# Resident embedding tables as float32 lookups in a DLRM tower: twelve tables, eight for all tiles, four behind the first, one looped body

## The chip, the core and the metric

The kernel runs on one core of a Trainium2 chip. The metric is the device time of one execution in microseconds. Three executions of the kernel before took 177.21, 178.31 and 182.38 us, with a median of 178.31 us. TensorE (PE) multiplies, VectorE (DVE) and ScalarE (ACT) work element by element and empty the PSUM banks, GpSimd (POOL) issues the indirect gathers, and SyncE (SP) issues the plain loads.

## The reference

For 512 samples, 26 ids pick one row of 128 float32 values each from 26 tables (eight tables of 1,000 rows, nine of 1,250, eight of 12,500, one of 125,000). With the dense row that makes 27 vectors a sample. All 351 pairwise products of them, and the dense features twice, go through a small network:

```
e = stack([tbl_0[ids[:, 0]], ..., tbl_25[ids[:, 25]]], axis=1)          # 512 x 26 x 128
combined = concatenate((dense[:, None, :], e), axis=1)                  # 512 x 27 x 128
inter = einsum('bfd,bgd->bfg', combined, combined)[:, iu, ju]           # 512 x 351, pairs f < g
h = concatenate([dense, inter, dense], axis=1)                          # 512 x 607
h = maximum(h @ W_top1 + b_top1, 0)      # 607 x 512
h = maximum(h @ W_top2 + b_top2, 0)      # 512 x 256
y = h @ W_top3                           # 256 x 1
```

## The kernel before

The batch is worked in four tiles of 128 samples. Each tile needs its 27 vectors with the features on the partitions (`xT`, two buffers). They come from two sources.

**Gathered tables.** For 19 tables, GpSimd issues one indirect load a table and tile (L260, 76 in all): 128 rows into `emb`. TensorE turns each by a transpose (L297), and DVE or ACT copies it into `xT` (L420 to L423, L501).

**Resident tables.** Seven small tables lie whole in SBUF (`table`, 125 partitions of 8 rows). A lookup is a product of table rows with a one-hot mask. SP loads each table's ids broadcast to 125 partitions (L232) and then the table itself (L233), in turn for the seven. ACT casts the ids (L537), DVE compares them with each partition's row number (L432, 8 masks a table), and DVE splits the table exactly into three bfloat16 parts (L449 `rest`, L454 `low`). TensorE adds three passes of 8 bfloat16 products (L284), and ACT keeps the result in `known` (L527). `LOOKUPS` gives the order: the seven tables for the first tiles before tile 0, and six shorter lookups for the remaining samples between the steps of tiles 0 to 2.

A tile then runs so: 128 small products of 32 x 32 (L342), interrupted by transposes of the next tile and by the dense part of layer 1 (L308); DVE transposes in blocks (L470), DVE and ACT pick the pairs (L477, L560), TensorE turns them three times (L361), and layer 1 (L308, 12 products), layer 2 (L385, 8) and the last layer (L393, 2) follow. `FILL` says between which of these steps the next tile's transposes stand. `keep_busy` (L316) multiplies the identity by itself to keep TensorE running. All code is unrolled; the order on each engine is the order in which it is written.

## Time and profile before

| | |
|---|---|
| time, median of three | 178.31 us |
| span of the profiled execution | 136.7 us |
| what lies around the span (median less span) | 41.6 us |
| first product of tile 0 | 64.67 us |
| first product of tile 1 | 85.26 us |
| first product of tile 3 | 121.42 us |
| last copy of the result | 134.83 us |
| TensorE busy | 104.4 us |
| GpSimd busy, with 76 gathers | 79.7 us |

The profile shows one execution from the first to the last instruction of the program. The profiled execution's own device time is not recorded, so the median of the three stands for it, and the 41.6 us around the span are a difference of two executions. A product of float32 operands stands in the trace as two instructions of TensorE, one of bfloat16 operands and a transpose as one. Products overlap in the array, so their pace is read from the distance of their starts, not from the duration of one.

### The profile page before, as it was taken

To read this page: it belongs to the slowest core of one execution; us is meant where nothing else is said; L and a number is where in the kernel's file an instruction comes from. 1 tells how busy PE (TensorE), PEld (TensorE's weight loads), DVE (VectorE), ACT (ScalarE), POOL (GpSimd) and SP (SyncE) were. 2 spreads that over 40 slices of the span, in tenths; PEclk is the share of its full clock that TensorE was granted. 3 is DMA by queue.
4 is the path that set the end of the run, shared out by engine and by line. 5 is a ranking of instruction groups with operands and counts; after the bars stand their busy time and mean duration, and the time that the engine had idled before them with its cause. 6 is when DMAs were issued, how large, how long until landed. Compare 5 with 4: busy or idle time off the path is not lost.

```text
span 136.7 us, 3746 instructions
## 1 busy us (share of the span) xinstructions
PE 104.4 (76%) x1660; PEld 79.8 (58%) x1660; DVE 54.4 (40%) x134; ACT 31.9 (23%) x71; POOL 79.7 (58%) x84
## 2 busy tenths in 40 slices
PE   5606999694739849079749999969999399986594
PEld 5502344242315626057639998858987399766592
DVE  0076758584855346179322032240411314113211
ACT  4010103030302005551000383004730023530211
POOL 6777887878778787778777777777772000000000
PEclk9985699999986986856985699999999869999999
DMA  2544444444448787744212212222221000000000
GB/s 43 103 167 145 164 148 152 158 151 164 150 163 252 192 218 196 174 136 142 79 46 62 58 48 53 62 58 50 50 64 44 0 5 0 0 5 5 5 0 1
DMA packets 5866, 12.68 MB, mean 93 GB/s; under 512 B 1636, under 2 KB 2148, under 8 KB 5850
## 3 DMA queue, kind: packets, MB, share of 16 engines
q1 hardware_dynamic: 3274, 7.45, 17.0%
q0 software_dynamic: 2432, 4.99, 14.6%
q8 instruction: 13, 0.21, 0.6%
q10 hardware_dynamic: 144, 0.01, 0.1%
q14 instruction: 3, 0.02, 0.1%
HBM read 12.43 MB, written 0.00 MB: 91 GB/s over the span
## 4 chain that ended last, share of the span: by engine, by line
PE 45%; SPq 21%; DMA 17%; issue 10%; ACT 5%; DVE 1%; ACTq 0%
DMA ids_i<-in_resident_ids 17%; SPq L233 12%; PE bank L308 12%; SPq L232 9%; PE prod L342 9%; PE prod L284 6%; PE prod L385 5%; PE bank L284 5%; PE bank L297 5%; ACT xT L544 1%; PE bank L393 1%; ACT xT L513 1%; PE prod L361 1%; PE bank L316 1%; PE bank L361 1%
## 5 line engine op out<-in xcount | busy, mean ns | idle before, releaser
L260 POOL DMA_INDIRECT emb<-in_tbl,ids_sb x76 | 77.7, 1022 | 23.1 <-issue 22.5
L284 PE MATMUL prod<-mask,table 125*128 125x512 bf16 (+3 forms) x80 | 15.9, 352 | 18.3 <-issue 12.7
L432 DVE TENSOR_SCALAR mask<-ids_h,col_sb 125x512 bf16<-125x512 f16 (+1 forms) x72 | 19.1, 344 | 11.5 <-ACT ids_h L537 11.5
L284 PEld LDWEIGHTS prod<-mask,table 125*128 125x128 bf16 x80 | 7.4, 109 | 25.6 <-issue 17.0
L284 PE MATMUL prod<-mask,rest 125*128 125x512 bf16 (+3 forms) x80 | 15.9, 354 | 0.2 <-DVE rest L449 0.2
L449 DVE TENSOR_TENSOR rest<-table 125x1024 f32<-125x1024 f32 (+1 forms) x8 | 8.6, 1091 | 15.4 <-DMA table<-in_tbl 15.4
L537 ACT CAST ids_h<-ids_i 125x512 f16<-125x512 int32 x7 | 4.3, 618 | 44.6 <-DMA ids_i<-in_resident_ids 44.6
L342 PE MATMUL prod<-xT 128*32 128x32 f32 x1024 | 12.4, 199 | 2.9 <-issue 2.4
L284 PE MATMUL prod<-mask,low 125*128 125x512 bf16 (+3 forms) x80 | 14.0, 326 | 0.0
L342 PEld LDWEIGHTS prod<-xT 128*32 128x32 f32 x1024 | 10.6, 109 | 4.7 <-issue 3.3
L284 PEld LDWEIGHTS prod<-mask,rest 125*128 125x128 bf16 x80 | 8.2, 116 | 7.0 <-issue 2.8
L308 PE MATMUL bank<-pairs,w1p_sb 117*128 117x128 f32 x96 | 12.1, 286 | 0.0
L297 PE MATMUL bank<-ident,emb 128*128 128x128 f32 x76 | 12.1, 297 | 0.0
L308 PEld LDWEIGHTS bank<-pairs,w1p_sb 117*128 117x128 f32 x96 | 11.9, 204 | 0.0
L284 PEld LDWEIGHTS prod<-mask,low 125*128 125x128 bf16 x80 | 7.7, 108 | 5.0 <-DVE low L454 0.2
L470 DVE STREAM_TRANSPOSE inter_s<-prod 128x288 f32<-128x288 f32 (+1 forms) x8 | 4.6, 612 | 14.4 <-PE prod L342 14.4
L297 PEld LDWEIGHTS bank<-ident,emb 128*128 128x128 f32 x76 | 10.0, 158 | 0.4 <-issue 0.2
L454 DVE TENSOR_TENSOR low<-rest 125x1024 bf16<-125x1024 f32 (+1 forms) x8 | 8.6, 1090 | 0.6
L513 ACT COPY xT<-known 128x896 f32<-128x896 f32 (+1 forms) x4 | 7.5, 1872 | 3.3 <-DMA known<-in_dense_t 3.3
L316 PE MATMUL bank<-ident 128*128 128x128 f32 x28 | 5.8, 374 | 3.1 <-issue 1.6
L385 PE MATMUL prod<-h,w_sb 128*128 128x128 f32 x64 | 7.9, 276 | 0.0
L385 PEld LDWEIGHTS prod<-h,w_sb 128*128 128x128 f32 x64 | 7.5, 192 | 0.1
(46 smaller groups left out, 77.9 us busy)
## 6 DMA issues: line engine op xcount, KB each, us to landing
table<-in_tbl SPq DMA_DIRECT2D x7, 500.0 KB
ids_i<-in_resident_ids SPq DMA_DIRECT2D x7, 250.0 KB
emb<-in_tbl,ids_sb POOLq DMA_INDIRECT x76, 3.6
w1p_sb<-in_w_pairs SPq DMA_DIRECT2D x1, 702.0 KB
w1d_sb<-in_w_dense SPq DMA_DIRECT2D x1, 512.0 KB, 20.8
w_sb<-in_w SPq DMA_DIRECT2D x1, 512.0 KB
known<-in_dense_t SPq DMA_DIRECT2D x1, 256.0 KB, 22.2
ids_sb<-in_ids SPq DMA_DIRECT2D x1, 38.0 KB, 2.1
```

What stands on the lines that cost most here:

```text
L232: sp.dma_start(ids_i[:, r, :], resident_ids[r].partition_broadcast(part_rows)).then_inc(s_idb[r], 16)
L233: sp.dma_start(table[:, r, :], resident[r].rearrange("(p k) d -> p (k d)", k=ROWS_PER_PART)).then_inc(s_table[r], 16)
L260: nc.gpsimd.indirect_dma_start(out=emb[:, t % 2, f, :], out_offset=None, in_=gathered[f], in_offset=bass.IndirectOffsetOnAxis(ap=ids_sb[:, ...
L284: mm = nc.tensor.matmul(look_dst(n), src[:, k, :], mask[:, r % KEPT, k, samples], start=(part == 0 and k == 0), stop=(part == 2 and k == R ...
L297: mm = nc.tensor.transpose(t_bank[g][:, i * P:(i + 1) * P], emb[:, t % 2, f, :], ident[:])
L308: return nc.tensor.matmul(l1_bank[n // 2][:, (n % 2) * P:(n % 2 + 1) * P], weights[:, n * P:(n + 1) * P], x, start=(weights is w1_sum and ...
L342: mm = nc.tensor.matmul(prod[SLOT_PITCH * q:SLOT_PITCH * (q + 1), i, :], x, x, start=True, stop=True)
L385: mm = nc.tensor.matmul(l2_bank[m][:, 0:P], w2_sb[:, c, m * P:(m + 1) * P], h1[:, c, :], start=(c == 0), stop=(c == HID1 // P - 1))
L432: nc.vector.tensor_scalar(mask[:, r % KEPT, k, samples], ids_h[:, r % 2, samples], col_sb[0:part_rows, ROW_ID + k:ROW_ID + k + 1], None, A ...
L449: nc.vector.tensor_tensor(by_row(rest[:, r % KEPT, :])[:, ks], by_row(table[:, r, :])[:, ks], upper_halves(table[:, r, :])[:, ks], ALU.sub ...
L454: nc.vector.tensor_tensor(low[:, r % KEPT, ks], by_row(rest[:, r % KEPT, :])[:, ks], upper_halves(rest[:, r % KEPT, :])[:, ks], ALU.subtra ...
L513: nc.scalar.copy(slots(t, 0, n), known[:, 0:n, t * P:(t + 1) * P].rearrange("d f (q j) -> d q j f", q=QUADS)).then_inc(s_pack_known, 1)
```

## The change

Twelve small tables are resident instead of seven: the eight of 1,000 rows (`EARLY`) and four of 1,250 rows (`LATE`), padded to whole rows of 128 partitions. The early eight are looked up for all 512 samples before tile 0. The late four are gathered by GpSimd for tile 0 and looked up for the other 384 samples at the end of tile 0. Fourteen tables stay gathered, so there are 18 gathers for tile 0 and 14 for each other tile, 60 in all.

A lookup multiplies the float32 table rows by a float32 mask: 8 products a table (10 for a late one), with no split of the table. After the first two tables, tables go in pairs, and one mask instruction of DVE serves both. The ids of the first six tables are loaded as six rows, and six products with a broadcast identity spread them over the partitions; ACT copies the result out of PSUM to int16. The ids of the other six come by a broadcast load.

TensorE's work of a tile is a loop body that is run four times, with branches for what differs between tiles. `xT` has one buffer instead of two, products are 27 x 27, all of a tile's products stand in one run, and the weights come in one load.

```diff
-RESIDENT = 7
...
+EARLY, LATE = 8, 4
+RESIDENT = EARLY + LATE
...
+COLUMNS = LATE + GATHERED
+FIRST_SLOT = 1 + EARLY
+
+FIRST_GROUPS = [(0, 4), (4, 4), (8, 4), (12, 4), (16, 2)]
+LATER_GROUPS = [(4, 4), (8, 4), (12, 3), (15, 2), (17, 1)]
+NG = 5
...
+
+PAIRS = [(r, r + 1) for r in range(0, RESIDENT, 2)]
+EARLY_PAIRS = EARLY // 2
+MASKS = 6
 
...
-WARM_UP = 9
-BUSY_BEFORE_PAIRS, BUSY_AMONG_PAIRS = 2, 3
+EARLY_GROUPS = [[0], [1], [2, 3], []]
...
+SPREAD = 6
...
+WARM_UP, WARM_KEEP = 2, 4
...
-            for r in range(RESIDENT):
-                sp.dma_start(ids_i[:, r, :], resident_ids[r].partition_broadcast(part_rows)).then_inc(s_idb[r], 16)
-                sp.dma_start(table[:, r, :], resident[r].rearrange("(p k) d -> p (k d)", k=ROWS_PER_PART)
-                             ).then_inc(s_table[r], 16)
-            sp.dma_start(known[:, 0, :], dense_t).then_inc(s_dense, 16)
-            sp.dma_start(w1d_sb[:], w1_dense.rearrange("(c p) n -> p c n", p=P)).then_inc(s_w1d, 16)
-            sp.dma_start(w1p_sb[0:K_PAIRS], w1_pairs.rearrange("(k p) n -> p k n", p=K_PAIRS)).then_inc(s_w1p, 16)
-            sp.dma_start(w2_sb[:], w2.rearrange("(c p) n -> p c n", p=P)).then_inc(s_w2, 16)
-            sp.wait_ge(s_y, TILES)
+            n = single * D
+            for r in range(2):
+                sp.dma_start(resident(r), early[0][:, r * n:(r + 1) * n]).then_inc(s_table[r], 16)
+            for b in range(1, EARLY_PAIRS):
+                if 2 * b == SPREAD:
+                    sp.dma_start(ids_h[:, SPREAD:, :], other_ids.partition_broadcast(P)).then_inc(s_other_ids, 16)
+                    sp.dma_start(known[:, 0, :], dense_t).then_inc(s_dense, 16)
+                sp.dma_start(table[:, b, 0:2 * n_rows[2 * b] * D], early[b]).then_inc(s_table[1 + b], 16)
+            sp.dma_start(w_sb[:], weights).then_inc(s_w, 16)
+            for r in range(EARLY, RESIDENT):
+                sp.dma_start(resident(r), late[r - EARLY].rearrange("(p k) d -> p (k d)", p=P)
...
+                        pool.wait_ge(s_tr, NG * (t - 2) + turned[-1] + 1)
+                    for c in range(first, first + n):
                         nc.gpsimd.indirect_dma_start(
-                            out=emb[:, t % 2, f, :], out_offset=None, in_=gathered[f],
-                            in_offset=bass.IndirectOffsetOnAxis(ap=ids_sb[:, t, f:f + 1], axis=0),
-                        ).then_inc(s_gather[t % 2][g], 16)
+                            out=rows(t, c), out_offset=None, in_=gathered[c],
+                            in_offset=bass.IndirectOffsetOnAxis(ap=ids_sb[:, column + c:column + c + 1], axis=0),
+                        ).then_inc(s_gather[t % 2][g] if t else s_gather_first[g], 16)
...
-            def look_up(n):
...
-                pe.wait_ge(s_table[r], 16)
-                for part in range(3):
-                    src = [upper_halves(table[:, r, :]), upper_halves(rest[:, r % KEPT, :]), low[:, r % KEPT]][part]
-                    for k in range(ROWS_PER_PART):
...
-                        mm = nc.tensor.matmul(look_dst(n), src[:, k, :], mask[:, r % KEPT, k, samples],
-                                              start=(part == 0 and k == 0),
-                                              stop=(part == 2 and k == ROWS_PER_PART - 1))
-                mm.then_inc(s_look, 1)
+            def look_up_first():
+
+                for r in range(2):
+                    pe.wait_ge(s_table[r], 16)
+                    for k in range(single):
+                        pe.wait_ge(s_mask, r * single + k + 1)
+                        nc.tensor.matmul(looked(r), resident(r)[:, k * D:(k + 1) * D], made_single(r, k),
+                                         start=(k == 0), stop=(k == single - 1)).then_inc(s_used, 1)
+
+            def look_up(b):
+
+                n = n_rows[2 * b]
+                pe.wait_ge(s_table[1 + b], 16 if b < EARLY_PAIRS else 32)
+                for k in range(n):
+                    step = first_step[b] + k
+                    pe.wait_ge(s_mask, masks_to(step + 1))
+                    for r in PAIRS[b]:
+                        mm = nc.tensor.matmul(looked(r), resident(r)[:, k * D:(k + 1) * D],
+                                              made(step, b)[:, r % 2, :], start=(k == 0), stop=(k == n - 1))
+                    mm.then_inc(s_used, 1)
...
+                with nc.tensor.If(p == 2):
+                    for g in some:
+                        bank_free(g)
+                        pe.wait_ge(s_gather[0][g], 16 * LATER_GROUPS[g][1])
+                        turn(2, g)
+                with nc.tensor.Else():
+                    with nc.tensor.If(p < TILES):
+                        for g in some:
+                            bank_free(g)
+
+                            pe.wait_ge(s_gather[1][g], (p + 1) * (8 * LATER_GROUPS[g][1]))
+                            turn(1, g)
...
+            pe.wait_ge(s_ident, 1)
+            keep_busy(WARM_UP)
+
+            pe.wait_ge(s_row_of, 1)
+            pe.wait_ge(s_id_exact, 1)
+            for r in range(SPREAD):
+                nc.tensor.matmul(id_bank[r][:], row_of[:, r, :], id_exact[:], start=True, stop=True
+                                 ).then_inc(s_spread, 1)
+            keep_busy(WARM_KEEP)
+            look_up_first()
...
+            for b in range(EARLY_PAIRS):
+                if b >= 2:
+
+                    pe.wait_ge(s_known, 2 * b - 2)
+                if b >= 1:
+                    look_up(b)
+                for g in EARLY_GROUPS[b]:
+                    turn_first(g)
+
+            pe.wait_ge(s_known, 6)
+            pe.wait_ge(s_w1sum, 1)
+            dense_part(slice(0, P))
+            turn_first(NG - 1)
+
+            with nc.tensor.Fori(1, TILES + 1) as p:
+
+
+                pe.wait_ge(s_ready_act, p)
+                pe.wait_ge(s_ready_dve, p)
...
                     for q in range(QUADS):
-                        x = xT[:, t % 2, i, q, :]
-                        mm = nc.tensor.matmul(prod[SLOT_PITCH * q:SLOT_PITCH * (q + 1), i, :], x, x,
+                        x = xT[:, i, q, 0:SLOTS]
+                        mm = nc.tensor.matmul(prod[SLOT_PITCH * q:SLOT_PITCH * q + SLOTS, i, 0:SLOTS], x, x,
                                               start=True, stop=True)
                 mm.then_inc(s_prod, 1)
...
+                turn_next(p, (0, 1))
...
+                turn_next(p, (2, 3))
...
+                with nc.tensor.If(p < TILES):
+                    dense_part(bass.ds((p % TILES) * P, P))
+                turn_next(p, (4,))
+                with nc.tensor.If(p == 1):
+
+                    pe.wait_ge(s_pack[2], 2)
+                    pe.wait_ge(s_pack[3], 2)
+                    pe.wait_ge(s_h2_act, 1)
+                    pe.wait_ge(s_h2_dve, 1)
+                    for b in range(EARLY_PAIRS, len(PAIRS)):
+                        look_up(b)
+
+                    pe.wait_ge(s_known, 8)
...
+                nc.vector.tensor_scalar(made_single(r, k), ids_h[:, r, :], col_sb[:, row:row + 1], None,
+                                        ALU.is_equal).then_inc(s_mask, 1)
+
+            def make_mask(b, k):
+                step = first_step[b] + k
+                if step >= MASKS:
+                    dve.wait_ge(s_used, masks_to(step - MASKS + 1))
+                row = row_id[n_rows[2 * b]] + k
+                nc.vector.tensor_scalar(made(step, b), ids_h[:, 2 * b:2 * b + 2, samples(b)],
+                                        col_sb[:, row:row + 1], None, ALU.is_equal).then_inc(s_mask, 1)
...
-                for ks in parts:
-                    nc.vector.tensor_tensor(by_row(rest[:, r % KEPT, :])[:, ks], by_row(table[:, r, :])[:, ks],
-                                            upper_halves(table[:, r, :])[:, ks], ALU.subtract
-                                            ).then_inc(s_rest, 2 // len(parts))
-                for ks in parts:
-                    dve.wait_ge(s_rest, 2 * r + (1 if ks.stop < ROWS_PER_PART else 2))
-                    nc.vector.tensor_tensor(low[:, r % KEPT, ks], by_row(rest[:, r % KEPT, :])[:, ks],
-                                            upper_halves(rest[:, r % KEPT, :])[:, ks], ALU.subtract
-                                            ).then_inc(s_low, 2 // len(parts))
...
+                    dve.wait_ge(s_other_ids, 16)
+                    dve.wait_ge(s_w, 16)
+                    nc.vector.tensor_tensor(w1_sum[:], w_sb[:, W1D:W1D + HID1], w_sb[:, W1D + HID1:W1D + 2 * HID1],
+                                            ALU.add).then_inc(s_w1sum, 1)
```

TensorE's program ahead of tile 0, before (`prod` and `bank` are PSUM, `mask` the one-hot operand, `table`, `rest` and `low` the three parts of the resident rows):

```order
L316 MATMUL bank<-ident 128x128 x9
L284 MATMUL prod<-mask,table 128x512 x8
L284 MATMUL prod<-mask,rest 128x512 x8
L284 MATMUL prod<-mask,low 128x512 x8
...
L284 MATMUL prod<-mask,table 128x384 x8
...
L297 MATMUL bank<-ident,emb 128x128 x16
...
L284 MATMUL prod<-mask,table 128x256 x8
```

and now, up to the loop (`id_exact` and `row_of` are the ids and the broadcast identity):

```order
L341 MATMUL prod<-ident 128x128 x2
L349 MATMUL bank<-id_exact,row_of 128x512 x6
L341 MATMUL prod<-ident 128x128 x4
L281 MATMUL bank<-mask,table 128x512 x16
L299 MATMUL bank<-ident,emb 128x128 x4
L292 MATMUL prod<-mask,table 128x512 x16
...
L299 MATMUL bank<-ident,emb 128x128 x8
L292 MATMUL prod<-mask,table 128x512 x16
L330 MATMUL bank<-known,w_sum 128x128 x4
L299 MATMUL bank<-ident,emb 128x128 x2
```

Where 24 bfloat16 products made a lookup there are 8 float32 ones, all of 512 columns, 64 in this stretch. On TensorE, from tile 0's products on, before (tile 1's round):

```order
L342 MATMUL prod<-xT 32x32 x64
L284 MATMUL bank<-mask,table 128x128 x8
L284 MATMUL bank<-mask,rest 128x128 x8
L284 MATMUL bank<-mask,low 128x128 x8
L361 MATMUL bank<-ident,pairs_s 117x128
...
L385 MATMUL prod<-h,w_sb 128x128 x8
L297 MATMUL bank<-ident,emb 128x128 x7
L393 MATMUL bank<-h,col_sb 1x128 x2
```

and now the end of the loop body (the first branch leads past what stands under it unless the pass is that of tile 0):

```order
L412 COMPARE_AND_BRANCH
L292 MATMUL bank<-mask,table 128x384 x20
L292 MATMUL prod<-mask,table 128x384 x20
L412 UNCONDITIONAL_BRANCH
L424 MATMUL bank<-h,col_sb 1x128 x2
L369 REGISTER_ALU
L369 COMPARE_AND_BRANCH
```

The lookups that lay in short pieces between the steps of tiles 0 to 2 are now one block of 40 products behind tile 0's layer 2. SP's queue, before (from its second load) and now:

```order
L232 DMA ids_i<-in_resident_ids 125x512
L233 DMA table<-in_tbl 125x1024
...
L235 DMA known<-in_dense_t 128x512
L236 DMA w1d_sb<-in_w_dense 128x2x512
L237 DMA w1p_sb<-in_w_pairs 117x3x512
L238 DMA w_sb<-in_w 128x4x256
```

```order
L239 DMA table<-in_early 128x1024 x2
L244 DMA table<-in_early 128x2048 x2
L242 DMA ids_h<-in_other_ids 128x3072
L243 DMA known<-in_dense_t 128x512
L244 DMA table<-in_early 128x2048
L245 DMA w_sb<-in_weights 128x3584
L247 DMA table<-in_late 128x1280 x4
```

The loads that went to 125 partitions go to 128, and the broadcast of the ids shrinks from seven loads to one.

## Rows read from the trace of the kernel before

**Rows 1.** The page: span, and busy time of each engine.
```profile
span 136.7 us, 3746 instructions
PE 104.4 (76%) x1660; PEld 79.8 (58%) x1660; DVE 54.4 (40%) x134; ACT 31.9 (23%) x71; POOL 79.7 (58%) x84
```
**Rows 2.** Chain that ended last, in order of time: start us, length us, what.
```profile
30.08 22.72 DMA ids_i<-in_resident_ids
...
64.67 0.69 PE prod L342 x46
...
121.42 1.34 PE prod L342 x87
...
134.83 0.25 ACT y_row L578
```
**Rows 3.** Windows: stretch, length, engines busy, PEclk, DMA share, GB/s.
```profile
6.00:36.00 30.00, 21.58 (x92) 9.33 (x93) 20.00 (x43) 4.31 (x8) 23.60 (x22) 0.89 0.46 157
42.00:45.00 3.00, 3.00 (x15) 1.60 (x14) 1.57 (x7) 1.00 (x2) 2.25 (x3) 0.72 0.92 268
```
**Rows 4.** Timeline: the start of TensorE's work (start us, us, engine, line).
```profile
1.52 4.21 PE L316 MATMUL bank<-ident 128*128 128x128 f32 x18 [1.52 <-POOL ident L248]
...
11.31 3.17 PE L284 MATMUL prod<-mask,table 125*128 125x512 bf16 x7 [5.58 <-DMA table<-in_tbl]
```
**Rows 5.** Timeline, TensorE: bfloat16 lookups of 512 and of 384 columns.
```profile
18.98 1.89 PE L284 MATMUL prod<-mask,table 125*128 125x512 bf16 x8
20.70 1.89 PE L284 MATMUL prod<-mask,rest 125*128 125x512 bf16 x8
...
34.06 1.46 PE L284 MATMUL prod<-mask,rest 125*128 125x384 bf16 x8
35.38 1.48 PE L284 MATMUL prod<-mask,low 125*128 125x384 bf16 x8
```
**Rows 6.** Timeline: 128 columns in bfloat16, float32, one-column weights (last: its group).
```profile
100.28 0.61 PE L284 MATMUL prod<-mask,rest 125*128 125x128 bf16 x8
100.73 0.61 PE L284 MATMUL prod<-mask,low 125*128 125x128 bf16 x8
...
129.19 2.84 PE L308 MATMUL bank<-pairs,w1p_sb 117*128 117x128 f32 x24
...
133.98 0.38 PE L393 MATMUL bank<-h,col_sb 128*1 128x128 f32 x2
...
L393 PE MATMUL bank<-h,col_sb 128*1 128x128 f32 x16 | 2.7, 271 | 0.1
```
**Rows 7.** The gathers: their group on the page, the first and the last one.
```profile
L260 POOL DMA_INDIRECT emb<-in_tbl,ids_sb x76 | 77.7, 1022 | 23.1 <-issue 22.5
...
3.10 1.10 POOL L260 DMA_INDIRECT emb<-in_tbl,ids_sb  x1 [0.28 <-DMA ids_sb<-in_ids]
...
102.70 0.94 POOL L260 DMA_INDIRECT emb<-in_tbl,ids_sb  x1 [0.30 <-issue]
```
**Rows 8.** TensorE's instruction loads, and stretches of the chain with nothing waited for.
```profile
q8 instruction: 13, 0.21, 0.6%
...
105.75 2.35 issue
...
122.77 1.26 issue
...
126.24 1.63 issue
```
**Rows 9.** DVE and ACT by line and form: busy us, mean ns.
```profile
L432 DVE TENSOR_SCALAR mask<-ids_h,col_sb 125x512 bf16<-125x512 f16 x40 | 12.4, 380 | 8.7 <-ACT ids_h L537 8.7
L454 DVE TENSOR_TENSOR low<-rest 125x1024 bf16<-125x1024 f32 x6 | 7.4, 1225 | 0.6
L527 ACT COPY known<-prod 128x512 f32<-128x512 f32 x3 | 1.7, 578 | 0.0
L513 ACT COPY xT<-known 128x896 f32<-128x896 f32 x2 | 3.5, 1762 | 3.3 <-DMA known<-in_dense_t 3.3
```

More of the change, by code:

```diff
@@ L311, in layer1, with dense_part @@
                                         skip_group_check=True)
+            def dense_part(samples):
+                for n in range(HID1 // P):
+                    layer1(n, w1_sum, known[:, 0, samples], False)
             def keep_busy(n):
                 for _ in range(n):
[L316 to L322 removed]
@@ L517, in pack_straight @@
-            def pack_straight(t):
-                act.wait_ge(s_look, STRAIGHT[t] + 1)
-                nc.scalar.copy(slots(t, RESIDENT, 1), look_dst(STRAIGHT[t])[:, 0:P].rearrange(
-                    "d (f q j) -> d q j f", f=1, q=QUADS)).then_inc(s_pack_known, 1)
-            def keep(n):
-                r, first, end, _ = LOOKUPS[n]
-                act.wait_ge(s_look, n + 1)
-                nc.scalar.copy(known[:, 1 + r, first * P:end * P], look_dst(n)).then_inc(s_known, 1)
+                nc.scalar.copy(*pack(t, g)).then_inc(s_ready_act if g == 3 and t >= 2 else s_pack[g], 1)
@@ L541, in _ @@
-            for r in sorted(EARLY_GROUPS):
-                for g in EARLY_GROUPS[r]:
-                    act.wait_ge(s_tr, g + 1)
-                    nc.scalar.copy(*pack(0, g, 0 if g == NG - 1 else None)).then_inc(s_pack[g], 1)
-                    if g == NG - 1:
-                        nc.scalar.copy(*pack(0, g, 1)).then_inc(s_pack_end, 1)
-                if r == RESIDENT - 3:
-                    keep(RESIDENT - 2)
+            nc.scalar.activation(table_load[0:1, 1:2], table_load[0:1, 0:1], ACT.Relu).then_inc(s_y, 1)
@@ L629 @@
     out = nc.dram_tensor("out_y", (BATCH, 1), F32, kind="ExternalOutput").ap()
-    build(nc, aps["dense_t"], aps["ids"], aps["resident_ids"], [aps[f"tbl_{f}"] for f in small],
-          [aps[f"tbl_{f}"] for f in large], aps["w1_pairs"], aps["w1_dense"], aps["w2"], aps["columns"], out)
+    late = [aps[f"late{i}"] for i in range(LATE)]
+    build(nc, aps["dense_t"], aps["ids"], aps["spread_ids"], aps["other_ids"],
+          [aps[f"early{b}"] for b in range(EARLY_PAIRS)], late, late + [aps[f"tbl_{f}"] for f in large],
+          aps["weights"], aps["columns"], out)
     r = run_bass_kernel_spmd(nc, [sent], core_ids=[0])
```

500 lines of the change are left out of this document (239 added, 261 removed).

## Prediction

> **What bounds the kernel now.** I read the totals first. TensorE is busy 104.4 of 136.7 us and GpSimd 79.7 us [rows 1]. Neither fills the span, so the chain of waits comes next [rows 2]. It has two parts. Up to tile 0's products at 64.67 us it runs through SP's loads, with 22.72 us on one broadcast of ids alone. From 64.67 to 134.83 us it stays on TensorE almost throughout. So the front is bound by loads and the tiles by TensorE and its hand-overs. The windows say why the loads are slow [rows 3]. From 6 to 36 us all transfers move 157 GB/s at a share of 0.46 of the 16 DMA engines. Between 42 and 45 us they move 268 GB/s at 0.92. Gathers take 128 rows of 512 bytes every (102.70 − 3.10) / 75 = 1.33 us [rows 7], which is 49 GB/s. SP's own part is therefore 108 GB/s in the first window and 219 in the second. GpSimd is not the bound: its last gather is issued at 102.70 us, and tile 3's products start at 121.42 us [rows 2, 7].
>
> **The price of a float32 lookup.** Warm bfloat16 lookups of 512 columns start 8 in 20.70 − 18.98 = 1.72 us, 0.215 us each. At 384 columns it is (35.38 − 34.06) / 8 = 0.165 us [rows 5]. At 128 columns bfloat16 takes (100.73 − 100.28) / 8 = 0.056 us, and float32 takes two instructions at (2.84 − 0.27) / 23 = 0.112 us, or 0.223 us a product [rows 6]. The factor is 4.0. No float32 product of more than 128 columns is in the trace. I take four times the bfloat16 price: 0.86 us at 512 columns, 0.66 us at 384. The lower bound is half of that. A table then costs 8 x 0.86 = 6.9 us where 24 x 0.215 = 5.2 us stood.
>
> **Front: from the start to tile 0's products, 64.7 us now.**
> - Start of the lookups. TensorE now starts warm-up at 1.52 us and waits for a table until 11.31 us [rows 4]. The new path is: six rows of ids land, a cast on DVE, a spreading product, an ACT copy out of PSUM of about 0.58 us, a mask of 0.38 to 1.23 us [rows 9], and on TensorE six spreading products (0.2 to 1.7 us each, nothing nearer than rows 5 and the cold 4.21 us for 18 instructions in rows 4) and four products to keep it busy. I put the first lookup at 8.0 us, between 6.3 and 9.7. The first table is half a megabyte second in the queue and lands before that.
> - 64 products of 0.86 us: 55.0 us.
> - 18 transposes at 0.11 us, the pace of a float32 instruction: 2.0 us.
> - TensorE's clock starts at the lower of its two levels, 1.2 GHz: the 18 float32 instructions of the warm-up stand (4.21 − 0.27) / 18 = 0.22 us apart [rows 4], twice the warm pace. I add 1.0 us for a stretch of lookups at that level, 0 to 4.
> - After the last lookup ACT and DVE take 128 samples and keep 512 (0.58 us [rows 9]), and pack the last group. The dense part runs beside that: 1.5 us.
>
> Sum 67.5 us, **+2.8 us**. The loads are hidden. SP must deliver 7.1 MB up to and with the merged weights, on which DVE waits before the masks of the fourth pair. At 219 GB/s that is 33 us and some latency, and TensorE needs those masks at 8.0 + 48 x 0.86 + 1.8 = 51 us. The masks are hidden too: one for a pair covers 1,024 elements, at most 1.23 us as the split of 1,024 elements [rows 9], against 1.72 us of products. Dropping the two splits of seven tables removes 14 x 1.23 = 17 us of DVE that only followed the loads, worth nothing of its own.
>
> The loads' price hangs on one point. The tables go to 128 partitions instead of 125. The slow window is the one in which the 125-partition loads run at 0.46 of the engines, the fast one has more engines at work [rows 3]. The Trainium skill (DMA: Bandwidth & Descriptors, "Why a DMA increments its semaphore by 16 and not by 1") says that a load uses the largest number of engines up to 16 that divides its partitions. By that rule 125 partitions use 5 engines and 128 use 16, and the windows agree with it: 5/16 is 0.31, and the rest of 0.46 is gathers. Without the rule, the 7.1 MB would come at 108 GB/s, the case of the late weights below.
>
> **Tiles without late lookups.** Tile 3 now takes 134.83 − 121.42 = 13.4 us, less 0.64 us for the dense products in it: 12.8 us. It has no transposes for a next tile, so it is the model for each tile. Its two stretches with nothing waited for (1.26 and 1.63 us [rows 8]) stay in it. They go with TensorE's instruction loads: 13 loads for 3,320 recorded instructions, one for 255 [rows 1, 8]. The loop body has about 650 that run in a pass, so I keep them. Tiles 0 to 2 add 6 transposes off any cover (0.7 us; the other 8 hide behind the block transposes), the dense part (4 x 0.223 = 0.9 us), and 0.4 us since ACT packs seven known slots (1.76 us [rows 9]) ahead of layer 1's activation: +2.0 us each. The three jumps back cost 1.2 us each, a shorter one of the stalls in rows 8, since the last layer waits on DVE meanwhile. One buffer of `xT` costs nothing: packing starts after the products and is over before the last layer ends. Sum 4 x 12.8 + 3 x 2.0 + 3 x 1.2 = 60.8 us against 70.2 us now: **−9.4 us**, which is the six lookups that lay between the steps and the waits around them.
>
> **Late lookups.** 40 products of 0.66 us are 26.4 us, with nothing else on TensorE, since they stand in one block before tile 0's last layer. DVE's 20 masks of 768 elements are at most 0.92 us against 1.32 us, six of them made ahead. Then come one take and one keep: 0.9 us. **+27.3 us**. What they replace is 12 gathers, 16 us of GpSimd. GpSimd already has slack, so this is worth nothing. With 60 gathers it ends at about 3 + 60 x 1.33 = 83 us.
>
> **Sum.** 136.7 + 2.8 − 9.4 + 27.3 = 157.4 us of span. With the 41.6 us around it the time is **199 us**, 20.7 us above the median of 178.31 us. A change within 2% (174.7 to 181.9 us) is about what cannot be told from none here.
>
> **Rivals.**
> - *The loop body stays loaded.* Then three passes lose no time to instruction loads: 3 x (2.9 + 1.2) = 12.3 us less, **187 us**. Against it: the 13 loads spread over the whole run show that little is held at a time. The Trainium skill (Runtime: NRT & Kernel Launch, "Instruction fetch mechanics") speaks against the loop: a taken branch to code outside a two-block window forces a fetch. By it each jump back costs at least a fetch; no branch of this kind is in the trace. Chance 0.13.
> - *Faster: wide float32 products take half.* The place is each lookup, the price 0.43 us. The 0.112 us between float32 instructions of 128 columns could be the weight load and not the streaming. It would have to be hidden behind 512 columns. Then the masks bind: 16 x 0.6 + 24 x 1.23 = 39 us in front instead of 55 (−16), and 14 masks of 0.92 us in the late block instead of 26.4 (−13). The time would be **171 us**. Against it: with weights of one column the two instructions still start 0.38 − 0.27 = 0.11 us apart [rows 6]. The Trainium skill (TensorE: Matmul & The Clock Gate, "LDWEIGHTS (loading the stationary operand)") gives columns / 1.2 ns, 107 ns for 128, which would account for the pace of layer 1 but not for that row. It decides below about 0.5 us a product. Chance 0.07.
> - *The weights come late.* At 108 GB/s they land at 68 us, and the fourth pair starts at 70 instead of 52 us: **217 us**. Chance 0.07.
> - *What lies around the span shrinks* with a program of TensorE a third as long. If it fell by half of 41.6 us the time would be near **179 us**. Nothing in the trace shows that it depends on it. Chance 0.06.
>
> **Chances and range.** My forecast has 0.60, and 0.07 is left for what I have not thought of, 0.04 of it slower and 0.03 faster. Around 199 the start gives ±1.7, the clock −1 to +3, the stalls −3 to +6, masks or hand-overs up to +4. The range goes on to the resident loop below, and towards the shrunken surround and the late weights: 180 to 215 us. Faster by over 2%: 0.07 + 0.03 = 0.10. Within 2%: 0.08, the surround and a little of the resident loop. Slower: 0.82.
>
> **What would show it.** Float32 lookup instructions starting 0.43 us apart, 0.33 in the late block; the first lookup near 8 us and the last early one near 66; tile 0's products at about 67.5, tile 1's about 42 us later; a block of 26 us before tile 0's last layer with the gathers long done; stretches with nothing waited for at the head of each pass. I am wrong if those starts are nearer than 0.4 us, if DVE's masks or the weights hold the lookups, or if a pass without late lookups takes other than 12 to 17 us.

## The result, and the profile after

The changed kernel takes **160.8 us** (median of 6, 160.18 to 161.77), the kernel before it 181.15 us (median of 6, 177.21 to 182.46): ratio **0.905**, 95% interval 0.900 to 0.910. It is faster by 9.5%, where I had forecast 199 us and a slowdown. A ratio is formed without executions that are over 1.5% above the fastest of their kernel, so it can differ from the quotient of two medians. One more thing has to be known to read any number below: the same kernel before takes about 180 us in some comparisons (called the 180-us kind below) and about 137 us in others (the 137-us kind), even with one chip number. The trace from which I predicted [rows 1] is of the second kind, while the runs beside it were of the first.

The page of the changed kernel: span, engines, how busy TensorE was in each 40th of the span (9 is 90% or more), TensorE's instruction queue, two groups.

```profile
span 158.9 us, 3443 instructions
PE 135.7 (85%) x1530; PEld 86.3 (54%) x1530; DVE 59.2 (37%) x112; ACT 31.6 (20%) x68; POOL 67.8 (43%) x66
...
PE   4999999999999999938973009999999889989695
...
q8 instruction: 4, 0.07, 0.2%
...
L268 POOL DMA_INDIRECT emb<-in_tbl,ids_sb x56 | 62.2, 1111 | 24.9 <-issue 16.9
...
L517 DVE TENSOR_SCALAR h<-prod,col_sb 128x128 f32<-128x128 f32 x4 | 1.4, 352 | 15.7 <-remote 11.8
```

Against [rows 1, 8]: TensorE has more work (135.7 for 104.4 us), 4 instruction loads in place of 13, and two idle slices in the middle. The profiled execution took 160.69 us, its span 158.9: there are **1.8 us** around it (the surround below), not 41.6. That holds for every run below.

The chain of the same execution, in order of time (start us, length us, what), answers to [rows 2]:

```profile
8.31 14.90 PE bank L281 x32
23.65 13.73 PE prod L292 x32
37.82 13.74 PE bank L292 x32
...
72.18 2.68 PE prod L378 x205
77.56 4.22 another core or an unknown queue
82.88 11.73 another core or an unknown queue
95.34 15.09 PE bank L292 x40
110.42 12.91 PE prod L292 x40
124.27 2.36 PE prod L378 x144
...
135.62 2.36 PE prod L378 x144
...
146.96 2.36 PE prod L378 x144
```

The front is one unbroken run of lookups. The three later passes are 11.35 and 11.34 us apart. Tile 0 holds two waits, 4.22 and 11.73 us, for something that no engine's record explains; the next view shows the second.

Timeline of all engines there (start us, us, engine, line; in brackets what ended the idle time):

```profile
83.46 1.06 PE L330 MATMUL bank<-known,w_sum 128*128 x8
...
84.84 0.94 POOL L268 DMA_INDIRECT emb<-in_tbl,ids_sb  x1 [0.30 <-issue]
86.08 0.95 POOL L268 DMA_INDIRECT emb<-in_tbl,ids_sb  x1 [0.30 <-issue]
...
91.09 0.95 POOL L268 DMA_INDIRECT emb<-in_tbl,ids_sb  x1 [0.30 <-issue]
93.89 0.37 ACT L597 ACTIVATE h<-prod,col_sb 128x128 f32<-128x128 f32 x1 [10.22 <-remote]
...
94.63 0.35 DVE L517 TENSOR_SCALAR h<-prod,col_sb 128x128 f32<-128x128 f32 x1 [11.75 <-remote]
```

Layer 2's products, on which both ACT and DVE wait, were over before 84 us. The two engines go on at 93.89 and 94.63, after GpSimd has stopped issuing gathers (the last before the pause ends at 92.04). By this record TensorE's signal arrived some 10 us late.

### The profile page after: what moved, and what is told of

The parts are those of the page before. It is cut to its first block, busy times and chain, and to the rows that moved or that the text cites. A ratio compares the mean times of both kernels' runs of the same rounds, so it can differ in the third digit from the quotient of the medians.

```text
span 158.9 us, 3443 instructions
## 1 busy us (share of the span) xinstructions
PE 135.7 (85%) x1530; PEld 86.3 (54%) x1530; DVE 59.2 (37%) x112; ACT 31.6 (20%) x68; POOL 67.8 (43%) x66
## 4 chain that ended last, share of the span: by engine, by line
PE 76%; another core or an unknown queue 10%; DVE 7%; issue 4%; DMA 1%; ACT 1%; ACTq 0%
PE prod L292 24%; PE bank L292 18%; PE bank L281 9%; PE prod L378 7%; PE bank L330 6%; PE prod L405 4%; DVE inter_s L495 3%; PE bank L299 2%; PE bank L349 2%; PE prod L341 1%; PE bank L424 1%; DMA id_rows<-in_spread_ids 1%; DVE xT L433 1%; PE prod L387 1%
## 5 line engine op out<-in xcount | busy, mean ns | idle before, releaser
L268 POOL DMA_INDIRECT emb<-in_tbl,ids_sb x56 | 62.2, 1111 | 24.9 <-issue 16.9
L448 DVE TENSOR_SCALAR mask<-ids_h,col_sb 128x1024 f32<-128x1024 int16 (+1 forms) x44 | 30.9, 707 | 39.4 <-PE bank L292 17.0
L292 PE MATMUL prod<-mask,table 128*128 128x512 f32 (+1 forms) x104 | 40.9, 551 | 0.0
L292 PE MATMUL bank<-mask,table 128*128 128x384 f32 (+1 forms) x72 | 29.0, 564 | 10.7 <-DVE h L517 10.7
L292 PEld LDWEIGHTS prod<-mask,table 128*128 128x128 f32 x104 | 19.6, 190 | 19.6 <-issue 13.9
L292 PEld LDWEIGHTS bank<-mask,table 128*128 128x128 f32 x72 | 14.5, 204 | 24.1 <-issue 19.7
L281 PE MATMUL bank<-mask,table 128*128 128x512 f32 x32 | 15.1, 633 | 0.0
L378 PE MATMUL prod<-xT 128*27 128x27 f32 x1024 | 11.1, 200 | 4.0 <-issue 2.9
L330 PE MATMUL bank<-pairs,w_sb 117*128 117x128 f32 x96 | 11.4, 275 | 0.0
L330 PEld LDWEIGHTS bank<-pairs,w_sb 117*128 117x128 f32 x96 | 11.0, 192 | 0.0
L281 PEld LDWEIGHTS bank<-mask,table 128*128 128x128 f32 x32 | 6.5, 208 | 7.9 <-issue 7.5
```

The source lines that it names most:

```text
L268: nc.gpsimd.indirect_dma_start(out=rows(t, c), out_offset=None, in_=gathered[c], in_offset=bass.IndirectOffsetOnAxis(ap=ids_sb[:, column + ...
L281: nc.tensor.matmul(looked(r), resident(r)[:, k * D:(k + 1) * D], made_single(r, k), start=(k == 0), stop=(k == single - 1)).then_inc(s_use ...
L292: mm = nc.tensor.matmul(looked(r), resident(r)[:, k * D:(k + 1) * D], made(step, b)[:, r % 2, :], start=(k == 0), stop=(k == n - 1))
L330: return nc.tensor.matmul(l1_bank[n // 2][:, (n % 2) * P:(n % 2 + 1) * P], weights[:, n * P:(n + 1) * P], x, start=(weights is w1_sum and ...
L378: mm = nc.tensor.matmul(prod[SLOT_PITCH * q:SLOT_PITCH * q + SLOTS, i, 0:SLOTS], x, x, start=True, stop=True)
L448: nc.vector.tensor_scalar(made(step, b), ids_h[:, 2 * b:2 * b + 2, samples(b)], col_sb[:, row:row + 1], None, ALU.is_equal).then_inc(s_mas ...
```

## Where the 40 us come from

The kernel before, unchanged, in a comparison of the 180-us kind (`before_again`):

> The kernel before, unchanged, to see the span of every execution beside its time. Theory A: about 42 us lie around the span in each execution (span 137, time 178 to 182), so they are outside what the trace shows. Theory C: the profiled execution with a span of 136.7 us was an unusual one, and the ordinary ones have spans near 177 us, with 2 us around them as in the changed kernel (158.9 of 160.7).

It took 182.34 us (median of 4, 179.15 to 182.73), profiled span 180.9 us with a time of 182.73 us. So theory C holds and theory A falls: the 40 us are inside the span. Timeline of TensorE there, the second eight products of a lookup, which start within 1.72 us in [rows 5]:

```profile
33.76 0.63 PE L284 MATMUL prod<-mask,rest 125*128 125x512 bf16 x1
35.32 0.59 PE L284 MATMUL prod<-mask,rest 125*128 125x512 bf16 x1 [0.92 <-issue]
38.10 0.59 PE L284 MATMUL prod<-mask,rest 125*128 125x512 bf16 x1 [2.20 <-issue]
40.21 0.58 PE L284 MATMUL prod<-mask,rest 125*128 125x512 bf16 x1 [1.52 <-issue]
43.01 0.58 PE L284 MATMUL prod<-mask,rest 125*128 125x512 bf16 x1 [2.22 <-issue]
```

The eight products of this part start at 33.76 to 50.70 us, 16.9 us where 7 x 0.215 = 1.5 are due. From the second on the starts are 2.1 or 2.8 us apart, multiples of 0.70, and "issue" says that the engine waited for nothing recorded. The waits of that execution (engine, line, for whom: total us, times, longest):

```profile
PEld prod L284 <- issue: 41.2, 36, 6.8
ACT known L527 <- remote: 39.0, 3, 25.6
DVE xT L420 <- PE bank L297: 36.0, 2, 23.8
...
PE prod L342 <- issue: 28.5, 31, 3.4
POOL emb L260 <- PE bank L297: 27.4, 3, 16.2
```

Windows of the kernel before, first the execution that I predicted from, which is past most of tile 0 there, then this one, in which TensorE does nothing but tile 0's interaction products (stretch, length, busy us and count of PE, PEld, DVE, ACT, POOL, clock, DMA share, GB/s):

```profile
75.00:95.00 20.00, 18.49 (x399) 16.83 (x398) 5.13 (x13) 7.04 (x18) 15.09 (x16) 0.93 0.22 55
```
```profile
75.00:95.00 20.00, 3.87 (x53) 2.25 (x53) 0.00 (x0) 0.59 (x2) 13.24 (x14) 0.63 0.20 50
```

In 20 us TensorE does 53 matmuls for 399. The DMA share is about the same, 0.20 for 0.22, so the DMA engines are not fuller. The granted clock is lower, 0.63 for 0.93, but that is far from a factor of seven. GpSimd's gathers go on (14 for 16). No such stretch begins after the last gather (126.0 us), and between 58 and 68 us, where GpSimd itself waits 16.17 us for TensorE, the lookups run at full pace. Four times the slowing ends 1 to 5 us after GpSimd's last gather before a pause: at 56.3 us after 51.7, at 95.5 after 92.4, at 103.8 after 102.8, at 129.5 after 126.9. That made the gathers the suspect. The runs with the gathers left out test it.

**Gathers left out of either kernel** (nothing gathered, those rows set to zero once by GpSimd). First comparison, of the 137-us kind:

```
+            nc.gpsimd.memset(emb[:], 0.0).then_inc(s_fill, 1)
             pool.wait_ge(s_ids, 16)
-            for t in range(TILES):
+            for t in range(0):
...
-                pe.wait_ge(s_gather[t % 2][g], (t // 2 + 1) * 16 * len(LOAD_GROUPS[g]))
+                pe.wait_ge(s_fill, 1)
```

> The kernel before without its 76 indirect gathers: emb is filled with zeros once, and TensorE's transposes wait for that alone (the gathered tables are left out of the result; every TensorE, DVE and ACT instruction stays). Theory G (while GpSimd's gathers are issued, TensorE's instructions and its semaphores come through late, which is the 40 us between the span of 136.7 us that I predicted from and the ordinary 177 to 181): span 125 to 137 us. Rival F (TensorE waits for its own instruction loads or for the plain loads of tables, gathers play no part): span stays within 175 to 181 us.

> The changed kernel without its 60 gathers, in the same way (the gathered tables are left out of the result). Theory G: the slow stretch at 68 to 72 us and the late semaphores at 80 to 95 us go, so the span falls from 158.9 to about 145 us. Rival F: about 159 us.

The kernel before was at 137.07 us here. Without gathers it took 130.08 us (127.04 to 131.14), the changed one 147.50 us (ratio 1.082, 1.071 to 1.092). Repeated in another comparison of that kind (before at 137.53):

> The kernel before with its 76 gathers left out and the gathered rows set to zero. Theory (gathers are what slows TensorE's instructions in the slower condition): about 130 us in both conditions, so a ratio near 0.72 beside a kernel before of 180 us, and 0.95 beside one of 137. Rival (that condition slows TensorE whether or not there are gathers, for instance by its clock alone): 165 us or more beside a kernel before of 180.

> The changed kernel with its 60 gathers left out and the gathered rows set to zero. Theory (gathers slow TensorE's instructions): 146 to 149 us in both conditions, that is 12 to 15 us under the changed kernel where the kernel before takes 180 us, and no more than 3 us under it where the kernel before takes 137. Rival (that condition slows TensorE without gathers): within 4 us of the changed kernel in both.

126.78 us (ratio 0.935, 0.904 to 0.966) and 147.54 us (1.087, 1.076 to 1.098). None of these four could decide; the third comparison was of the 180-us kind (before at 180.69), though with the same chip number as the second:

> The kernel before with its 76 gathers left out (gathered rows zero). Beside a kernel before of about 180 us, theory (gathers are what slows TensorE there): 126 to 132 us, ratio near 0.72. Rival (TensorE is slowed there without gathers too): 165 us or more. Beside a kernel before of about 137 us both expect some 127 to 130 and nothing is told apart.

> The changed kernel with its 60 gathers left out (gathered rows zero). Beside a kernel before of about 180 us, theory: 146 to 149 us, which is 12 to 15 us under the changed kernel's 160.8. Rival: 157 us or more. Beside a kernel before of about 137 us both expect 147 to 148.

**130.86 us** (ratio **0.726**, 0.719 to 0.733) and **147.65 us** (0.820, 0.814 to 0.826). The theory holds and its rival falls: without gathers either kernel takes nearly the same in both kinds of comparison (the one before 126.8 to 130.9 us, the changed one 147.5 to 147.7). Gathers cost the kernel before 50 us there, and the changed one 13 against its 160.8 of another comparison (some 15, since filling the rows with zeros puts its first lookup at 10.48 instead of 8.11 us). TensorE's interaction products (1,024 instructions) show it. Their group in three executions: the kernel before at 182.73 us, then without gathers beside 180.69, then with the plain transfers of the next paragraph.

```profile
L342 PE MATMUL prod<-xT 128*32 128x32 f32 x1024 | 19.3, 217 | 28.5 <-issue 28.5
```
```profile
L344 PE MATMUL prod<-xT 128*32 128x32 f32 x1024 | 10.8, 198 | 4.0 <-issue 3.9
```
```profile
L340 PE MATMUL prod<-xT 128*32 128x32 f32 x1024 | 10.8, 198 | 3.3 <-issue 3.2
```

**What in a gather does it.** Each gather became a plain transfer of 128 rows that lie behind each other (the same 64 KB, other rows than the ids ask for), on GpSimd's queue and then (`sp.dma_start`, behind its loads) on SyncE's:

```
-                        nc.gpsimd.indirect_dma_start(
-                            out=emb[:, t % 2, f, :], out_offset=None, in_=gathered[f],
-                            in_offset=bass.IndirectOffsetOnAxis(ap=ids_sb[:, t, f:f + 1], axis=0),
-                        ).then_inc(s_gather[t % 2][g], 16)
+                        nc.gpsimd.dma_start(emb[:, t % 2, f, :], gathered[f][t * P:(t + 1) * P, :]
+                                            ).then_inc(s_gather[t % 2][g], 16)
```

> The kernel before with each of its 76 gathers replaced by a plain transfer of the same 64 KB, 128 rows in a row, issued on the same GpSimd queue (so the output is that of other rows). It tells something only where the kernel before takes about 180 us. Theory G (it is the software-made descriptors of GpSimd's queue that slow TensorE's instructions): still 165 to 182 us. Rival I (it is the indirect form alone, with a descriptor for each row from a list of ids): 126 to 140 us, as without gathers (130.9). Beside a kernel before of 137 us both expect 130 to 140.

> The same plain transfers, issued by SyncE behind its own loads (so the first come some 30 us later), and none by GpSimd. Theory G (GpSimd's software queue): 128 to 140 us in either condition. Rival T (any traffic of this size into these tiles beside TensorE slows it): 160 us or more beside a kernel before of 180 us.

The kernel before was at 179.97 us (170.46 to 182.74). They took **142.79 us** (142.21 to 143.97) and **143.23 us** (142.47 to 143.77). The first falls between the two expectations, close to rival I: queue, bytes and packets (2,432 of GpSimd's queue in both) are kept, and of the 49 us that the gathers cost there 37 are gone (28 even against the fastest execution of the kernel before, 170.46); the other 12 are about what they cost beside 137 us (7 to 11). Theory G in the form of these two expectations, that any transfer of GpSimd's queue does it, falls, and so does T, that any traffic does.

So the slowing needs the gather in its indirect form. What in it counts is not shown, because three things changed together: the list of ids, rows that lie scattered over a table instead of in a row, and the time of one issue, 0.54 us for 0.98. A GpSimd that is busy issuing is not enough, though. From 83.82 to 89.73 us of the first of these runs it issues 11 plain transfers without a pause, and beside them 128 of TensorE's interaction instructions take 1.30 us (at 88.48 us), as they do where GpSimd issues nothing (at 68.92 us).

## What the change is worth

**Both kernels in a comparison of the 137-us kind**, together with the variant without late lookups:

> The changed kernel, unchanged, beside the kernel before. The kernel before has so far taken 177 to 183 us in one comparison and 135 to 141 us in another. Theory (two conditions: in one of them TensorE's instructions come at one per some 0.70 us for stretches of up to 20 us while GpSimd issues gathers, and the kernel before suffers more of it than the changed one): if the kernel before lands at about 180 us, the changed one takes 160 to 162 us and shows stretches at about 68 to 72 and 83 to 94 us; if it lands at about 137 us, the changed one takes 147 to 151 us, ratio 1.07 to 1.10, without these stretches. Rival (the lookups as whole float32 operands and the loop save time in themselves, whatever the condition): a ratio of 0.89 to 0.92 in either case, so 123 to 126 us beside 137.

> The changed kernel with eight tables looked up and none of the four late ones: 18 gathers for every tile. It took 150.7 us where the kernel before took 180.8 (ratio 0.846). Theory (two conditions): beside a kernel before of about 137 us it takes 125 to 131 us, because 40 late products of 0.65 us fall away from a changed kernel of 147 to 151; beside one of about 180 us again 150 to 152. Rival (late lookups save as much as they cost): no faster than the changed kernel of the same comparison.

The kernel before took 137.53 us, the changed one **144.61 us** (143.65 to 145.72): ratio **1.069**, 1.048 to 1.090. There the change is slower, as forecast in sign, if a little less than the theory expected (147 to 151 us); its rival, a gain in either kind, falls. Windows of the changed kernel, this execution and then the measured one of 160.69 us, from tile 0's products to the start of the late block, and the late block:

```profile
67.70:80.40 12.70, 10.88 (x321) 10.08 (x322) 5.84 (x13) 4.83 (x11) 8.49 (x10) 1.00 0.20 50
80.40:106.30 25.90, 25.90 (x82) 15.05 (x80) 9.06 (x15) 1.32 (x3) 8.27 (x9) 1.00 0.09 23
```
```profile
67.70:79.00 11.30, 7.69 (x285) 6.92 (x286) 4.30 (x10) 2.60 (x6) 4.99 (x6) 0.85 0.12 29
79.00:95.30 16.30, 4.51 (x39) 4.08 (x37) 1.70 (x5) 2.23 (x6) 10.32 (x12) 0.81 0.18 48
95.30:123.30 28.00, 27.96 (x81) 16.10 (x82) 8.68 (x14) 1.32 (x3) 0.61 (x1) 0.93 0.01 2
```

Tile 0 takes 12.7 us before the block in one and 27.6 in the other. The block itself is 25.9 and 28.0 us (clock 0.93 for 1.00). These two differences are the whole 16.9 us between spans of 142.0 and 158.9. So the two kinds of comparison differ by 43 us for the kernel before and 16 for the changed one, and the 27 us between them turn +7 into −20.

**The late lookups.** `loop_no_late` and `loop_no_late_2` are one kernel, with 18 gathers for every tile, 72 in all, and no late block:

```
-EARLY, LATE = 8, 4
+EARLY, LATE = 8, 0
...
-LATER_GROUPS = [(4, 4), (8, 4), (12, 3), (15, 2), (17, 1)]
+LATER_GROUPS = FIRST_GROUPS
...
-                with nc.tensor.If(p == 1):
...
-                    for b in range(EARLY_PAIRS, len(PAIRS)):
-                        look_up(b)
```

> The changed kernel with the eight early tables alone resident and eighteen gathered for every tile (72 gathers), no lookup in the loop. By my sum the late block of 26 us goes, and the 10.7 us wait ahead of it if that belongs to the block: span 158.9 - 27 = 132 us, or 121 us; GpSimd's last gather is issued at about 3 + 72 x 1.33 = 99 us. Rival: the gathers bind, tile 3 waits for them, and the span stays above 140 us.

Beside a kernel before of 180.83 us: **150.68 us**, ratio 0.846 (0.835 to 0.857). Beside 137.53: **123.79 us**, ratio **0.910** (0.898 to 0.923), just under the expected 125 to 131. It beats both kernels in either kind. The late lookups cost 20.8 us net beside 137 us, and some 10 beside 180 (160.8 is of another comparison).

In the first of the two runs the span of 148.9 us missed my 132 or 121 and came out where the rival said, above 140, but not for its reason. TensorE's trace shows no wait for a gather. What holds it are sparse starts of the interaction products while gathers are issued: from 70 to 82.5 us in tile 0, and once again from about 98 to 112.8 in tile 1, where the gathers go on to 109.8 us.

The medians of the two kinds side by side, in us (not all of one column are of one comparison):

| | 137-us kind | 180-us kind |
|---|---|---|
| kernel before | 137.1, 137.5 | 180 to 182 |
| changed kernel | 144.6 | 160.8 |
| changed, no late lookups | 123.8 | 150.7 |
| before, without gathers | 130.1, 126.8 | 130.9 |
| changed, without gathers | 147.5, 147.5 | 147.7 |

**The loop.** Four passes written out instead of looped:

```
-            with nc.tensor.Fori(1, TILES + 1) as p:
+            for p in range(1, TILES + 1):
...
-                with nc.tensor.If(p == 2):
+                if p == 2:
...
```

> The changed kernel with TensorE's loop written out four times and its branches decided in the program; nothing else differs. Theory A (what lies around the span goes with the length of TensorE's straight program): span near 160 us, time near 200 us, as first forecast. Theory B (it goes with the loads, inputs or other engines): time within 2% of 160.8 us. If the 10 us in tile 0 in which the semaphores of layer 2 come late belongs to the loop or its branches, the span falls to about 149 us.

166.51 us (165.83 to 166.96), ratio 0.934 (0.920 to 0.947), some 5.7 us above 160.8, which is of another comparison. The span is 165.1 us. Theory A falls, and theory B's 2% are missed by little. Instruction loads and stretches of its chain with nothing waited for:

```profile
q8 instruction: 12, 0.20, 0.5%
```
```profile
119.11 2.01 issue
133.13 2.36 issue
149.11 2.29 issue
```

These are three stalls of 2.0 to 2.4 us at the interaction products of passes 2 to 4. An instruction load begins within a microsecond before each of them (in the microseconds from 118, 132 and 148 us). The looped kernel has 4 loads, the last begun before 79 us, in its first pass, and none of these stalls.

The 5.7 us understate what the loop saves. The slowing in tile 0 was milder in the unrolled execution, and its late block started at 88.85 us for 95.34:

```profile
88.85 14.99 PE bank L292 x40
```

From tile 1's products to the end of the span it takes 165.1 − 117.7 = 47.4 us, the looped kernel 158.9 − 124.3 = 34.6. So three passes in a loop are 12.8 us shorter. Not all of that is the stalls (6.7 us together); in passes 3 and 4 the unrolled kernel also takes 5.12 us for the 24 instructions of layer 1 that take 2.68 in the looped one, at a granted clock of 0.51 and 0.50 for 1.00. Whether the late signals belong to the loop is answered too: they come in the unrolled kernel as well (ACT 3.7 and DVE 7.1 us).

**Length of the program.** 520 float32 products that are never executed stand behind the loop:

```
+            with nc.tensor.Fori(1, 2) as q:
+                with nc.tensor.If(q == 5):
+                    keep_busy(520)
```

> The changed kernel with 520 float32 products behind the loop that a branch skips, so TensorE's program is longer and none of it more is executed. Theory A in the form that the stored length counts: time 180 to 200 us. Theory A in the form that only executed blocks count, and theory B: 161 us.

157.39 us (154.42 to 160.69), profiled 157.13 with a span of 155.3: 1.8 us around the span again. Nothing around the span depends on the program's length. That it came out at or below 160.8 us goes with a shorter slowing in tile 0, not with the padding as far as the trace shows: its late block starts at 91.24 us for 95.34, and the span is 155.3 us for 158.9.

**Float32 or bfloat16 lookups.** The kernel before with 8 whole float32 products a table and no split; and the changed kernel with three bfloat16 products on the upper halves for each float32 one (the lower parts of the values are left out):

```
-                for part in range(3):           # before_f32_lookups
+                for part in range(1):
-                    src = [upper_halves(table[:, r, :]), ...][part]
+                    src = by_row(table[:, r, :])
...
-    nc.tensor.matmul(looked(r), resident(r)[:, k * D:(k + 1) * D], ...)    # after_bf16_lookups
+    for part in range(3):
+        nc.tensor.matmul(looked(r), upper(r, k), ...)
```

> The kernel before with its lookups as 8 float32 products a table instead of 24 bfloat16 ones, the masks in float32 and no split of the tables on DVE; tables, order, gathers, loads and unrolled tiles stay. By the price of the products (4 x 0.215 against 3 x 0.215 us for 512 columns) it is 5 to 12 us slower than before. Theory G: a third fewer TensorE instructions stand in the stretch in which gathers are issued, so the lag shrinks and the time falls below 175 us.

> The changed kernel with each float32 lookup product replaced by three bfloat16 ones on the table's upper halves with a bfloat16 mask (the two lower parts of the split are left out, so the result has the rows' upper halves three times). By the price of the products it gains 64 x 0.215 + 40 x 0.165 = 20 us of TensorE: span about 139 us. Theory G: half as many TensorE instructions again in the same stretch, at twice the rate and more, so the lag comes back in the front and the span is 155 us or more.

Beside 137.07 us: 138.0 us (ratio 0.987, 0.973 to 1.001) and **126.28 us** (0.925, 0.917 to 0.933). In the kernel before the form of the lookup is worth nothing that shows, where I had expected 5 to 12 us more; the two numbers of theory G could not be tested beside 137 us. In the changed one TensorE is full, and the float32 form costs 144.6 − 126.3 = 18 us (the two are of two comparisons); three bfloat16 products take three quarters of one in float32, and a quarter of the 64 early and 40 late products' time (55 + 26 = 81 us) is 20.

> The kernel before with each lookup as eight whole float32 products in place of 24 in bf16, and no split on VectorE. Beside a kernel before of about 180 us, theory (the cost is the number of TensorE instructions issued while GpSimd issues gathers, at some 0.70 us each): 13 lookups lose 16 matmuls each, 208 matmuls and their weight loads, of which those in the slowed stretches go at 0.70 us or more apiece, so 150 to 172 us, a ratio of 0.83 to 0.95. Rival (the slowing is a delay of signals and not of instructions): a ratio of 0.97 to 1.01, as at 137 us.

Beside 180.69 us: 178.92, 180.23 and 171.18 us, too few and too far apart for an interval. The last lies within the theory's 150 to 172 us, but the kernel before has shown 170.46 us as well, so the times decide little. The trace tells more (chain, of the execution with 180.23 us):

```profile
39.22 17.89 another core or an unknown queue
57.77 7.53 PE prod L282 x16
```

Its first 24 wide float32 products start at 11.42 us and run without a gap, gathers or not. Then ACT waits 17.9 us, up to 57.1, for a lookup whose last product ended at 35.4 us, TensorE waits for ACT, and tile 0's products start at 74.75 us, against 78.30 in `before_again` and 64.67 in [rows 2]. So most of the loss moved from the starts of instructions to a late signal. What is lost is not simply 0.70 us for each instruction.

## Why the prediction was wrong, step by step

- **What failed: "With the 41.6 us around it".** I took the median of the runs shown (178.31) minus the profiled span (136.7) as a constant outside the span, and added it to the new span. All runs show 1.8 us there. The 41.6 us were 1.8 of surround and some 40 of a slowing *within* the span, which that profiled execution did not have. Being in the span it is not a constant: it was 43 us for the kernel before and 16 for the changed one. The traces suggest why, though no run tests it alone: where gathers are issued beside wide float32 products without a hand-over, nothing is lost, and the changed kernel's front is of that kind up to 66 us. A surround of 23% of the time should have been questioned; "it shrinks" was a rival at 0.06, with a wrong mechanism (`after_padded` and `after_unrolled` both have 1.8 us).
- **The span: 157.4 forecast, 142.0 in the execution of the same kind.** The measured 158.9 is close only by luck: 16.9 us of slowing make up for what follows.
- *Front*, 67.5: right. Tile 0's products start at 67.76 (67.88 in the measured run), the first lookup at 8.03 (8.11), forecast 8.0. One product takes 13.74 / 16 = 0.86 us as forecast. The rival of half the price falls. The weights weren't late: from 7.9 to 65.9 us the loads and gathers move 183 GB/s, and no lookup waits on them. (The sum of the rival with half the price is 170 us by its own terms, not 171.)
- *Late block*, +27.3: right for the block itself. 25.9 us for 40 products, 12.91 / 20 = 0.65 us a product. But the 12 gathers that it replaces were not "worth nothing": leaving out the block saved 20.8 us and not 26, since with 18 gathers a tile the passes of `loop_no_late_2` start 13.45 and 13.51 us apart for 11.34 and 11.35. That term was too small by some 5 us.
- *Tiles*, 60.8 us: **mis-sized by 14 us**. Measured 13.7 (tile 0) + 11.34 + 11.35 + 10.1 = 46.5. I kept the stalls at instruction loads in every pass and added 1.2 us for each jump back. Rival 1 was the truth: the body stays loaded. It priced that at 12.3 us, and the unrolled kernel's three passes are 12.8 us longer. It gave 157.4 − 12.3 = 145.1 us of span, 146.9 with the true surround, against 144.61 measured. One of my own signs of being wrong came true with it: a pass takes 11.34 us, where I had named 12 to 17. By the Trainium skill (Runtime: NRT & Kernel Launch, "Instruction fetch mechanics") a taken branch out of a two-block window forces a fetch; 4 loads of 16 KB in all, and passes without one, do not agree with it for TensorE. That the instruction memory of TensorE holds 2,048 instructions, as the same section of the Trainium skill says, does agree: a pass has some 650 recorded ones.
- **The rule on engines and partitions** (the Trainium skill, DMA: Bandwidth & Descriptors, "Why a DMA increments its semaphore by 16 and not by 1") held. From 10 to 20 us of the measured run the transfers move 401 GB/s at a share of 1.02, where everything together, with the loads to 125 partitions, made 157 at 0.46 [rows 3].

With the right surround and my own span I would have forecast 159 us beside a kernel before of 138.5: slower by 15%, where 7% was measured. Nothing in the trace shown could tell how the change fares in the other kind of comparison; the gap between 178.31 and 136.7 could tell that there is one.

## What to carry to other kernels

Set the profiled execution's own time beside its span first. If the median of the runs lies far above it, the profile shows another condition than the runs, and the gap is neither a constant nor outside the span. Where GpSimd's indirect gathers run beside short TensorE instructions, measure once with the gathers left out: what they cost was 7 us on one occasion and 50 on another in the same kernel. And once TensorE has no idle time left, every wide float32 product is paid for in full; here the late tables cost more than the gathers they replace in both kinds of comparison.

## What the runs showed that I had not expected

- One kernel at 137 and at 180 us, at 1.8 us around the span in both, the same chip number among them. During the slowed stretches TensorE starts an instruction, or a few, at multiples of 0.70 us, and its signals reach ACT and DVE some 10 us late. Once ACT waited 25.6 us, up to 56.4 us, for a lookup whose last product had ended at 24.1.
- Not every stretch with gathers is slowed: in the changed kernel's front 64 wide products keep their 0.86 us beside 40 gathers. What turns the slowing on, and why it differs from one comparison to the next, stays open. The runs show only that the indirect gathers have to be there, and that a stretch ends 1 to 5 us after they pause.
- A gather's pitch is 1.25 us beside an idle DVE, and 58 / 40 = 1.45 us on average in that front, beside DVE's masks.
